# Turning maxima, context and two normed inputs with 32x32 block transposes and DMA instead of TensorE

## Chip, cores and metric

One Trainium2 chip, one core. The metric is the device time of one launch in microseconds (us), lower is better. Engines are named TensorE (PE), VectorE (DVE), ScalarE (ACT), GpSimd (POOL) and SyncE (SP, which issues all DMAs here).

## What is computed

A decoder block in float32 on 64 sequences of 256 tokens with 256 features, 16 heads of 16. `ctx_1024` has 120 rows per sequence. Cut to what matters:

```python
def reference(x, ctx_1024, ...):                    # x (64, 256, 256), ctx (64, 120, 256)
    x = x + local_attention(_layernorm(x))          # each token sees 3 before and 3 after it
    x = x + cross_attention(_layernorm(x), ctx_1024, ctx_1024)
    h = _layernorm(x)
    h = h + causal_attention(rmsnorm(h, n1_w))
    h = h + moe(rmsnorm(h, n2_w))                   # softmax gate, silu(h @ up.T) @ down.T, width 1024
    return x + h
```

## The kernel before

Tokens lie on partitions in `x`, `y`, `xn` (two blocks of 128), features on partitions in `xT`, as the projections need them. The 64 sequences are independent. Five are under way at a time, each in a lane of its own (`LANES = 5`, one set of SBUF tensors per lane), so that TensorE can work for one while the others wait for other engines. Work is cut into named parts ("turn", "project", "max", ...), each on one engine.

**Parts of a sequence.** For each of the layers local (0), cross (1), causal (2) and feed-forward (3): "moments" (DVE, then POOL) and "norm" (ACT) make the normed input `xn`. "turn" transposes it: four 128x128 transposes on PE (L790) into PSUM, and an ACT copy to `xT` (L1028). The context is turned the same way by "turn_ctx" (L797, L1032) into `cT`. Local attention: "project_rows" (L810) for k, v, q, "send" and "fetch" through DRAM (L703, L719) to give each partition its window, products on POOL (L630, L635) and sums on DVE (L1361), "turn_out" (L925) and "project_out" (L939). Cross and causal attention: "project" (L832, L838), "max" (scores in one orientation on PE, L866, their maxima on DVE, L1407), "shift" (the maxima transposed on PE, L877, copied by DVE, L1411), "place" (two DMAs, L728, that write them as extra rows into `qT`), "scores" (L888, exponentials L1075), "values" (L911), "normalise" (DVE, L1418 to L1434, which turns blocks by itself) and "project_out". Feed-forward: "gate" (L950), "up" (L961), "down" (L970).

**Whole array and parts.** "max", "scores", "values" and "gate" use 32 rows or 32 columns of the PE array at a time (`tile_position`), four side by side. Everything else uses the whole array.

**What sets the order.** `Plan` makes the instruction order of each engine at build time, from durations written into the parts. On PE the order is that of the table `POSITION` (sequence number plus position), with free choice among the next 60 parts only in the fill and the drain. On the other engines a part that is ready is taken by its due time, shifted by the table `SHIFTED`. Each engine's queue is then fixed and in order. PSUM has 8 banks; parts on the array take four ("quad") or one ("single"). Where the plan sees PE wait over 1 us, it puts filler matmuls there, which compute nothing (L770):

```python
if now - stopped > LONG_WAIT and p.name != "derive":
    one = PASSING * (2 if warmth < WARMS_IN else 1)
    self.passing[p.name, n, p.args] = count = int((now - stopped - MARGIN) / one)
```

Of the kernel before, what the change touches and what calls it, by code (L numbers as in the profile page):

```python
# [7 lines left out]
P = 128  # L8
LANES = 5
# [8 lines left out]
DOTS = 6  # L18
SLOT = 32
# [39 lines left out]
def score_units(layer):  # L59
# [16 lines left out]
EASY_REJOIN = 0.13  # L76
WIRE = 330.0
LANDING = 1.1
COOLS_AFTER, WARMS_IN = 1.5, 3.4
EMPTIED = 0.24  # L80
# [3 lines left out]
EARLY = 0  # L84
EARLY_ON_DVE = {("window_times", (c,)): busy for c, busy in ((0, 0.92), (2, 0.65), (4, 0.65), (6, 0.8), (8, 0.7), (10, 0.7))}
BEHIND = {("weights", (3,), "SP"): ("fetch", ("k",), "SP", 0), ("weights", (4,), "SP"): ("fetch", ("v",), "SP", 0)}

POSITION = {("turn", (0,)): -0.0773, ("turn_ctx", ()): -0.0394, ("project_rows", ("k",)): -0.0389, ("project_rows",
    ("v",)): 0.0516, ("project_rows", ("q",)): 0.0643, ("project", (1, "v")): 0.8052, ("turn_out", ()): 1.0641,
    ("project_out", (0,)): 1.2473, ("project", (1, "k")): 1.2641, ("turn", (1,)): 1.4729, ("project", (1, "q")):  # L90
    1.5195, ("max", (1, 0)): 1.6554, ("max", (1, 1)): 1.6713, ("shift", (1,)): 1.8861, ("scores", (1, 1)): 1.9724,
    ("scores", (1, 0)): 2.0874, ("values", (1,)): 2.3718, ("project_out", (1,)): 2.5298, ("turn", (2,)): 2.6364,
    ("project", (2, "k")): 2.7808, ("project", (2, "q")): 2.8094, ("max", (2, 0)): 2.8523, ("project", (2, "v")):
    2.899, ("max", (2, 1)): 3.0514, ("max", (2, 2)): 3.1338, ("shift", (2,)): 3.2929, ("scores", (2, 1)): 3.4513,
    ("scores", (2, 0)): 3.53, ("scores", (2, 2)): 3.6057, ("values", (2,)): 3.8413, ("project_out", (2,)): 3.9289,
    ("turn", (3,)): 4.2641, ("up", (0,)): 4.3625, ("up", (1,)): 4.3677, ("gate", ()): 4.4232, ("up", (2,)): 4.4727,
    ("up", (3,)): 4.4907, ("down", ()): 4.6197}

SHIFTED = {("down", (), "DVE"): -0.0629, ("fetch", ("k",), "SP"): 0.2, ("fetch", ("v",), "SP"): 0.5928, ("gate", (),
    "ACT"): 0.0687, ("load", (), "SP"): -0.8911, ("max", (1, 0), "DVE"): -0.0311, ("max", (1, 1), "DVE"): 0.0013,  # L100
    ("max", (2, 0), "DVE"): -0.4475, ("max", (2, 1), "DVE"): 0.4429, ("max", (2, 2), "DVE"): 0.7354, ("moments",
    (0,), "DVE"): 0.6903, ("moments", (0,), "POOL"): 0.9004, ("moments", (1,), "DVE"): -0.981, ("moments", (1,),
    "POOL"): 0.2012, ("moments", (2,), "DVE"): 0.0297, ("norm", (0,), "ACT"): -0.0134, ("norm", (0,), "POOL"):
    -0.2814, ("norm", (1,), "POOL"): 0.12, ("norm", (2,), "ACT"): -0.393, ("norm", (3,), "ACT"): 1.0224, ("norm",
    (3,), "POOL"): 0.1706, ("normalise", (2,), "DVE"): -0.0553, ("place", (1,), "SP"): -0.3445, ("project", (1,
    "q"), "ACT"): -0.8017, ("project", (1, "v"), "DVE"): 0.247, ("project", (2, "k"), "ACT"): 0.6832,
    ("project_out", (0,), "DVE"): 0.4817, ("project_out", (1,), "DVE"): -0.2502, ("project_out", (2,), "DVE"):
    -0.1622, ("project_rows", ("k",), "DVE"): -0.078, ("project_rows", ("v",), "DVE"): -0.3457, ("scores", (2, 0),
    "ACT"): 0.3209, ("scores", (2, 1), "ACT"): -0.4329, ("scores", (2, 1), "POOL"): -0.4149, ("scores", (2, 2),
    "ACT"): -0.8947, ("scores", (2, 2), "POOL"): 0.336, ("send", ("k",), "SP"): 1.8199, ("send", ("v",), "SP"):  # L110
    -0.087, ("shift", (1,), "DVE"): 0.0251, ("shift", (2,), "DVE"): -0.9285, ("store", (), "SP"): -0.0128, ("turn",
    (0,), "ACT"): 0.1725, ("turn", (1,), "ACT"): 0.1889, ("turn", (2,), "ACT"): 2.029, ("turn_ctx", (), "ACT"):
    0.021, ("turn_out", (), "ACT"): -0.1453, ("up", (0,), "ACT"): 0.4114, ("up", (0,), "DVE"): -0.5841, ("up", (1,),
    "ACT"): 0.026, ("up", (1,), "DVE"): 1.7562, ("up", (2,), "ACT"): 0.1018, ("up", (2,), "DVE"): 0.0745, ("up",
    (3,), "ACT"): -0.0954, ("up", (3,), "DVE"): -0.1548, ("weigh", (), "POOL"): 0.0496, ("window_exp", (), "ACT"):
    -0.0668, ("window_max", (), "DVE"): -0.5864, ("window_reduce", (0,), "DVE"): -0.0766, ("window_reduce", (1,),
    "DVE"): 0.8292, ("window_reduce", (2,), "DVE"): 0.0141, ("window_reduce", (3,), "DVE"): -0.3849,
    ("window_reduce", (4,), "DVE"): -0.1917, ("window_reduce", (5,), "DVE"): -0.5257, ("window_reduce", (6,),
    "DVE"): 0.384, ("window_reduce", (7,), "DVE"): -0.0381, ("window_reduce", (8,), "DVE"): 1.1728,
    ("window_reduce", (9,), "DVE"): 0.1471, ("window_reduce", (10,), "DVE"): 1.2711, ("window_reduce", (11,),  # L120
    "DVE"): -0.0619, ("window_times", (0,), "POOL"): 0.052, ("window_times", (2,), "POOL"): -0.0118,
    ("window_times", (3,), "POOL"): 0.1314, ("window_times", (4,), "POOL"): 1.461, ("window_times", (5,), "POOL"):
# [1391 lines left out]
```

## Time and profile before

| | |
|---|---|
| median of 3 runs | 3522.82 us (3520.79 to 3526.21) |
| the profiled execution, its time | 3523.18 us |
| its span | 3521.5 us |
| PE busy | 3464.6 us (98%) |
| POOL busy | 2498.7 us (71%) |
| ACT busy | 1828.8 us (52%) |
| DMA, mean | 63 GB/s |
| granted clock | 0.999 |

A row of the timeline gives the start in us from the span's start, the length, engine, line, operation, output and inputs, shapes, and how many instructions it merges. A float32 matmul is recorded as two, so x8 is four matmuls. Matmuls overlap, and a row's length holds some of the next one's; the distance of two starts is what the work takes in the queue. In square brackets stands idle time of that engine before the row and what ended it.

### The profile page before, as it was taken

The page shows a single profiled execution, that of the slowest core. Times are in us where ns is not written, and L with a number is a line of the kernel's source. Part 1 is how long each engine was busy: PE and PEld are TensorE (multiplying, and loading weights), DVE is VectorE, ACT ScalarE, POOL GpSimd, SP SyncE. Part 2 cuts the span into 40 slices and gives each one's busy share as a digit, 9 for nine tenths or more (in the row PEclk, how much of TensorE's full clock was granted, in tenths as well). Part 3 has the DMA queues.
Part 4 walks back from the last instruction along what each step waited for, and adds up shares of the span by engine and source line. Part 5 has one row for each costly group of instructions (what it writes and reads, how often), then busy time and mean ns, then how long its engine had stood idle before and what let it go on. Part 6 is the DMA issues. An engine that isn't in the chain of part 4 may idle for free.

```text
span 3521.5 us, 92506 instructions
## 1 busy us (share of the span) xinstructions
PE 3464.6 (98%) x36557; PEld 2788.9 (79%) x36557; DVE 2674.4 (76%) x5867; ACT 1828.8 (52%) x4241; POOL 2498.7 (71%) x3160
## 2 busy tenths in 40 slices
PE   8899999999999999999999999999999999999998
PEld 5577888888888888888888888888888888888876
DVE  5677787787787787787787787787787787787763
ACT  3344555555555555555545545545545545545542
POOL 5767777777777777777777777777777777777731
PEclk9999999999999999999999999999999999999999
DMA  5111221121121121221121221221221121121200
GB/s 182 50 51 50 70 73 51 68 74 51 68 74 52 67 74 50 69 74 50 66 77 47 69 77 46 69 77 47 69 77 47 69 77 47 69 77 47 69 8 10
DMA packets 90151, 223.35 MB, mean 63 GB/s; under 512 B 9286, under 2 KB 56706, under 8 KB 73346
## 3 DMA queue, kind: packets, MB, share of 16 engines
q1 hardware_dynamic: 89730, 217.44, 18.1%
q8 instruction: 300, 4.92, 0.6%
q14 instruction: 121, 0.99, 0.1%
HBM read 164.92 MB, written 50.39 MB: 61 GB/s over the span
## 4 chain that ended last, share of the span: by engine, by line
PE 94%; POOL 2%; ACT 2%; DVE 2%; issue 1%; SPq 0%; DMA 0%; DVEq 0%; POOLq 0%; ACTq 0%
PE ps L970 13%; PE ps L961 13%; PE ps L832 11%; PE ps L810 10%; PE ps L888 9%; PE ps L939 9%; PE ps L866 9%; PE ps L911 8%; PE ps L838 5%; PE ps L790 3%; PE ps L860 1%; PE ps L877 1%; ACT prob L1075 1%; PE ps L925 1%; POOL chunks L635 1%; DVE nmax L1407 1%
## 5 line engine op out<-in xcount | busy, mean ns | idle before, releaser
L635 POOL TENSOR_TENSOR chunks<-v_windows,xT 128x560 f32<-128x560 f32 (+1 forms) x384 | 879.6, 2301 | 92.2 <-DVE xT L1382 89.2
L1407 DVE TENSOR_REDUCE nmax<-ps 128x4 f32<-128x480 f32 (+2 forms) x1280 | 776.9, 671 | 182.8 <-PE ps L866 182.6
L1075 ACT ACTIVATE prob<-ps 128x256 f32<-128x256 f32 (+2 forms) x1536 | 670.7, 556 | 457.7 <-PE ps L888 457.5
L630 POOL TENSOR_TENSOR chunks<-rest,k_windows 128x512 f32<-128x512 f32 (+1 forms) x384 | 552.2, 1455 | 373.9 <-DMA k_windows<-passed_on 301.1
L1361 DVE TENSOR_REDUCE held<-chunks 128x80 f32<-128x560 f32 (+1 forms) x384 | 294.6, 768 | 321.2 <-POOL chunks L635 319.8
L961 PE MATMUL ps<-xT,w_up 128*128 128x256 f32 x2048 | 480.3, 383 | 1.4 <-ACT xT L1028 1.3
L970 PE MATMUL ps<-w_down,held 128*128 128x256 f32 x2048 | 459.1, 382 | 1.1 <-DVE held L1460 1.0
L970 PEld LDWEIGHTS ps<-w_down,held 128*128 128x128 f32 x2048 | 383.8, 190 | 60.1 <-DVE held L1460 2.8
L961 PEld LDWEIGHTS ps<-xT,w_up 128*128 128x128 f32 x2048 | 372.4, 190 | 69.4 <-issue 20.6
L1232 POOL TENSOR_SCALAR_AFFINE_SELECT prob<-prob 128x512 f32<-128x512 f32 x512 | 311.3, 642 | 50.6 <-ACT prob L1075 50.6
L1028 ACT COPY xT<-ps 128x512 f32<-128x512 f32 x256 | 152.9, 597 | 361.6 <-PE ps L790 361.6
L1361 DVE TENSOR_REDUCE xT<-chunks 128x32 f32<-128x512 f32 (+1 forms) x384 | 291.9, 760 | 21.8 <-POOL chunks L630 21.7
L911 PE MATMUL ps<-prob,va 120*32 120x256 f32 (+2 forms) x6144 | 303.5, 346 | 4.2 <-ACT prob L1075 2.0
L911 PEld LDWEIGHTS ps<-prob,va 120*32 120x32 f32 (+1 forms) x6144 | 179.7, 110 | 122.4 <-issue 45.9
L866 PE MATMUL ps<-held 32*128 32x120 f32 (+2 forms) x4096 | 260.2, 321 | 3.2 <-ACT held L1045 2.4
L888 PE MATMUL ps<-held 32*128 32x128 f32 (+2 forms) x3072 | 241.4, 380 | 10.0 <-issue 4.6
L1204 POOL TENSOR_TENSOR x<-x,y 128x512 f32<-128x512 f32 x64 | 81.4, 1272 | 233.8 <-DVE y L1444 233.8
L1016 ACT ACTIVATE held<-x,nmean,rstd 128x256 f32<-128x256 f32 x256 | 140.0, 595 | 186.0 <-POOL nmean L1179 186.0
L1108 ACT ACTIVATE rest<-ps 128x512 f32<-128x512 f32 x256 | 154.7, 604 | 115.9 <-PE ps L961 115.9
L888 PEld LDWEIGHTS ps<-held 32*128 32x128 f32 (+1 forms) x3072 | 123.1, 181 | 97.2 <-issue 90.1
L1460 DVE SCALAR_TENSOR_TENSOR held<-rest,ps 128x512 f32<-128x512 f32 x256 | 172.7, 675 | 23.1 <-ACT rest L1108 22.4
L1418 DVE STREAM_TRANSPOSE ps<-ps 128x512 f32<-128x512 f32 x256 | 170.1, 707 | 20.0 <-PE ps L911 19.3
(152 smaller groups left out, 6783.8 us busy)
## 6 DMA issues: line engine op xcount, KB each, us to landing
k_windows<-passed_on SPq DMA_DIRECT2D x64, 1024.0 KB, 5.0
v_windows<-passed_on SPq DMA_DIRECT2D x64, 1024.0 KB, 5.0
x<-in_x SPq DMA_DIRECT2D x64, 256.0 KB, 2.9
passed_on<-rest SPq DMA_DIRECT2D x64, 256.0 KB, 2.3
passed_on<-held SPq DMA_DIRECT2D x64, 256.0 KB, 3.7
out<-x SPq DMA_DIRECT2D x64, 256.0 KB, 2.2
y<-in_ctx SPq DMA_DIRECT2D x64, 120.0 KB, 2.9
held<-nmaxT SPq DMA_DIRECT2D x256, 8.0 KB
```

The source lines that it names most:

```text
L630: return engine.tensor_tensor(chunk_of(c).rearrange("p (j d) -> p j d", d=D), token_rows["q"][s][:, b, :].unsqueeze(1).to_broadcast([P, n, ...
L635: return engine.tensor_tensor(chunk_of(c).rearrange("p (h i j) -> p h i j", i=HD, j=WINDOW), window("v", b * D + first * HD, (HD, n), (1, ...
L810: last = nc.tensor.matmul(ps[:, b, tb * D:(tb + 1) * D], tokens, W[f"local_{w}"][:, k, :], start=(k == 0), stop=(k == 1))
L832: last = nc.tensor.matmul(ps[:, b, m * n:(m + 1) * n], wt[:, k, m * P:(m + 1) * P], src[:, k, 0:n], start=(k == 0), stop=(k == 1))
L866: last = nc.tensor.matmul(ps[:, to[r], place * keys:(place + 1) * keys], qT[s][e][rows, m, tb * P:(tb + 1) * P], kT[L][s][e][rows, m, 0:keys],
L888: last = nc.tensor.matmul(ps[0:keys, to[r], n * qs:(n + 1) * qs], kT[L][s][e][rows, m, key0:key0 + keys], qT[s][e][rows, m, q0:q0 + qs], s ...
L911: last = nc.tensor.matmul(ps[SLOT * j:SLOT * (j + 1), b, e * T + q0:e * T + q0 + qs], va[s][0:keys, kb, head:head + SLOT], pr[0:keys, j, c ...
L961: last = nc.tensor.matmul(ps[:, b, m * T:(m + 1) * T], w_up[:, k, (2 * m2 + m) * P:(2 * m2 + m + 1) * P], xT[s][:, k, :], start=(k == 0), ...
L970: last = nc.tensor.matmul(ps[:, b, tb * D:(tb + 1) * D], hid[s][:, m, tb * P:(tb + 1) * P], w_down[:, m, :], start=(m == 0), stop=(m == F ...
L1075: last = nc.scalar.activation(prob_pair(seq, L, m)[0:keys, :, r, col:col + qs], of_pair, ACT.Exp, scale=SCALE)
L1361: nc.vector.tensor_reduce(to, chunk_of(c).rearrange("p (x i) -> p x i", i=width), AX_X, ALU.add).then_inc(reduced[s], 1)
L1407: nc.vector.tensor_reduce(of_heads[:, ms[0]:ms[-1] + 1, :, r], src, AX_X, ALU.max, negate=True).then_inc(emptied[b], 1)
```

## The change

- `BY_DMA = ("ctx", 1, 3)`: the context and the normed inputs of cross and feed-forward are no longer turned on PE. ACT writes the normed rows in 32-feature blocks. "flip" (DVE) transposes all 32x32 blocks in place. "spread" (SP) writes them to a DRAM tensor with features as rows, in 8 DMAs (4 for the context) whose pieces are 32 tokens, 128 B. "gather" (SP) waits for all of them and reads 256 features by 256 tokens back into `xT` (or `cT`) in one DMA. The turns of layers 0 and 2 stay on PE.
- "shift" loses its PE transpose: DVE writes the maxima into `max_blocks`, transposes its 32x32 blocks, and "place" takes 8 DMAs instead of 2.
- `POSITION` and `SHIFTED` are new, which gives every engine another order. Code for doing window products on DVE, which was switched off (`EARLY = 0`), is gone.

```diff
+BY_DMA = ("ctx", 1, 3)
+FLIP, SPREAD_KB = 0.56, 1000
...
-POSITION = {("turn", (0,)): -0.0773, ("turn_ctx", ()): -0.0394, ("project_rows", ("k",)): -0.0389, ("project_rows",
...
+POSITION = {("turn", (0,)): 2.982, ("project_rows", ("k",)): 3.1458, ("project_rows", ("v",)): 3.1965,
...
+    def by_dma(what, after, flip, hops, spread_kb, kb):
+        a = part("flip", (what,), "DVE", flip, after)
+        a = part("spread", (what,), "SP", hops * DMA_ISSUE, [a, of_ctx] if what == LOCAL and of_ctx else [a],
+                 lag=LANDING, kb=spread_kb)
+        return part("gather", (what,), "SP", DMA_ISSUE, [a], lag=LANDING, kb=kb)
...
-            a = through("shift", (layer,), 0.2, "DVE", 0.4, last)
-            shifted = part("place", (layer,), "SP", 2 * DMA_ISSUE, [a], lag=2.0)
+            a = part("shift", (layer,), "DVE", 0.2, last)
+            shifted = part("place", (layer,), "SP", 8 * DMA_ISSUE, [a], lag=1.6)
...
-                        wait_taken(sp, "shift", seq, L)
+                        sp.wait_ge(flipped[s], reached["flipped", "shift", seq, (L,)])
                         for e in range(2):
-                            to = qT[s][e][16 * (1 - e):P:32]
-                            sp.dma_start(to, nmaxT[s][8 * e:8 * e + 8, :]).then_inc(placed[s], 16)
+                            to = qT[s][e][16 * (1 - e):P:32].rearrange("r m (b i q) -> r m b i q", b=2, q=SLOT)
+                            for i in range(4):
+                                first = SLOT * i + 4 * e
+                                sp.dma_start(to[:, :, :, i, :], nmaxT[s][first:first + 4, :]).then_inc(placed[s], 16)
+                    elif name == "spread":
+                        what, = args
+
+                        sp.wait_ge(flipped[s], reached["flipped", "flip", seq, args])
...
+                            to = features[s].rearrange("(x f) t -> f x t", f=SLOT)
+                            for tb in range(2):
+                                for i in range(4):
+                                    first = tb * P + i * SLOT
+                                    sp.dma_start(to[:, :, first:first + SLOT], xn_blocks[s][SLOT * i:SLOT * (i + 1), :, tb]
+                                                 ).then_inc(spread[s], 16)
+                    elif name == "gather":
+                        what, = args
+
+                        sp.wait_ge(spread[s], reached["spread", "spread", seq, args])
...
+                            sp.dma_start(xT[s][:], features[s].rearrange("(k p) t -> p k t", p=P)).then_inc(gathered[s], 16)
...
-                    elif name == "shift":
-                        L, = args
-                        wait_taken(pe, "max", seq, L, len(max_fills(L, T, C)) - 1)
-                        b = bank(name, seq, args)
-                        for tb in range(2):
-                            last = nc.tensor.transpose(ps[0:H, b, tb * P:(tb + 1) * P], nmax[s][:, tb, :], ident[:])
-                        last.then_inc(filled[b], 1)
...
+                    elif name == "flip":
+                        what, = args
+                        if what == "ctx":
+                            dve.wait_ge(ctx_loaded[s], reached["ctx_loaded", "load", seq, ()])
+                            rows = cx[s]
+                        else:
+                            dve.wait_ge(xn_ready[s], reached["xn_ready", "norm", seq, (what,)])
+                            rows = xn_blocks[s].rearrange("p x b f -> p (x b f)")
+                        nc.vector.transpose(rows, rows).then_inc(flipped[s], 1)
...
-                        b = bank(name, seq, args)
-                        nc.vector.tensor_copy(nmaxT[s][:], ps[0:H, b, 0:T]).then_inc(emptied[b], 1)
+                        L, = args
+                        for f in range(len(max_fills(L, T, C))):
+                            wait_taken(dve, "max", seq, L, f)
+                        nc.vector.transpose(nmaxT[s][:], max_blocks[s][:].rearrange("p m b h -> p (m b h)")).then_inc(
+                            flipped[s], 1)
```

How the queues move is read from the orders. The numbers behind names are lanes. PE, a steady round before, from the causal maxima past the causal output projection (L939 with `xT0`; L877 is the shift, L790 a turn, L797 the context's turn):

```order
L866 MATMUL ps<-rest1,held1 128x128 x4
L877 MATMUL ps<-ident,nmax2 16x128 x2
L838 MATMUL ps<-w_causal_v,xT1 128x256 x4
L790 MATMUL ps<-ident,held4 128x128 x4
L939 MATMUL ps<-w_causal_o,xT0 128x256 x4
L797 MATMUL ps<-ident,y4 128x120 x2
L810 MATMUL ps<-w_local_k,xT4 128x256 x4
L888 MATMUL ps<-held2 120x256 x4
```

PE now, from the causal output projection of lane 4 (L991 is the old L939, L869 the old L810, L849 the old L790, L919 and L925 masks and maxima, L940 scores, L977 the old L925, L897 the old L838):

```order
L849 MATMUL ps<-ident,held3 128x128 x4
L991 MATMUL ps<-w_causal_o,xT4 128x256 x4
L869 MATMUL ps<-w_local_k,xT3 128x256 x4
L919 MATMUL ps<-mask_rows,pick_rows 128x4x32 x16
L925 MATMUL ps<-held0 128x128 x4
L925 MATMUL ps<-rest0,held0 128x128 x4
L925 MATMUL ps<-held0 128x128 x4
L925 MATMUL ps<-rest0,held0 128x128 x4
L897 MATMUL ps<-w_cross_v,y2 120x256 x2
L869 MATMUL ps<-w_local_v,xT3 128x256 x4
L977 MATMUL ps<-ident,held2 128x128 x4
L919 MATMUL ps<-mask_rows,pick_rows 128x2x32 x16
```

Behind these rows come maxima, one unit of scores, the local output projection, a unit of scores, masks and maxima, the local q projection and the cross values, and then the gate and "up" of lane 4. Before, a turn of lane 0 stood between the causal output projection and "up", and the gate came after half of "up". A round has one context turn, two turns and two shifts fewer on PE. It goes from whole-array work into parts eight times (one of them straight from rows to columns inside), six times before. The whole order has 1093 changes of this kind against 927, and 429 fillers against 328, of which 18 stood ahead of the first projection and none do now.

SP, one round before (L732 store, L696 and L697 load, L728 place, L703 send, L719 fetch):

```order
L732 DMA out<-x3 128x2x256
L696 DMA x3<-in_x 128x2x256
L697 DMA y3<-in_ctx_1024 120x256
L728 DMA held1<-nmaxT1 4x2x256 x2
L703 DMA passed_on<-rest3 128x512
L719 DMA k_windows<-passed_on 128x2048
L703 DMA passed_on<-held3 128x512
L719 DMA v_windows<-passed_on 128x2048
L728 DMA held0<-nmaxT0 4x2x256 x2
```

SP now, from the first place of a round to the store (L757 place, L775 spread, L785 gather, L789 store; load, the context's spread in 4 and its gather follow):

```order
L757 DMA held4<-nmaxT4 4x4x32 x8
L733 DMA passed_on<-rest1 128x512
L746 DMA k_windows<-passed_on 128x2048
L775 DMA features<-held2 32x8x32 x8
L733 DMA passed_on<-held1 128x512
L785 DMA xT2<-features 128x2x256
L746 DMA v_windows<-passed_on 128x2048
L757 DMA held3<-nmaxT3 4x4x32 x8
L775 DMA features<-held0 32x8x32 x8
L785 DMA xT0<-features 128x2x256
L789 DMA out<-x2 128x2x256
```

A round had 11 DMAs and has 46. The fetch of the v windows now stands behind the gather of a feed-forward input.

VectorE before, from the addition of the causal output (L1444) through its moments:

```order
L1444 TENSOR_TENSOR y0<-y0,ps 128x512
L1327 TENSOR_TENSOR rest4<-ps,b_local_k 128x512
L1316 BN_STATS stats0<-y0 128x6 x2
L1319 BN_AGGR mv0<-stats0 128x2 x2
L1407 TENSOR_REDUCE nmax1<-ps 128x2 x4
```

VectorE now, from the same addition (L1495) to the flip of that input (L1389):

```order
L1495 TENSOR_TENSOR y1<-y1,ps 128x512 [waits filled5]
L1376 BN_STATS stats1<-y1 128x6 [waits emptied5]
L1376 BN_STATS stats1<-y1 128x6
L1379 BN_AGGR mv1<-stats1 128x2 [waits dve_step]
L1379 BN_AGGR mv1<-stats1 128x2
L1396 TENSOR_TENSOR rest0<-ps,b_local_k 128x512 [waits filled4]
L1409 TENSOR_REDUCE held4<-chunks1 128x80 [waits multiplied4]
L1455 TENSOR_REDUCE max_blocks2<-ps 128x2x2 [waits filled0]
L1455 TENSOR_REDUCE max_blocks2<-ps 128x2x2 [waits filled1]
L1455 TENSOR_REDUCE max_blocks2<-ps 128x2x2 [waits filled2]
L1455 TENSOR_REDUCE max_blocks2<-ps 128x2x2 [waits filled3]
L1389 STREAM_TRANSPOSE held1<-held1 128x512 [waits xn_ready1]
```

The flip stands behind a window sum and four reductions of another lane's maxima.

## Rows read from the trace of the kernel before

**Rows 1.** The page: busy time by engine, and the chain that ended last.
```profile
PE 3464.6 (98%) x36557; PEld 2788.9 (79%) x36557; DVE 2674.4 (76%) x5867; ACT 1828.8 (52%) x4241; POOL 2498.7 (71%) x3160
...
PE 94%; POOL 2%; ACT 2%; DVE 2%; issue 1%; SPq 0%; DMA 0%; DVEq 0%; POOLq 0%; ACTq 0%
```

**Rows 2.** Timeline of PE, in the fill and in a steady round (start, length).
```profile
97.10 0.71 PE L888 MATMUL ps<-held 32*120 32x256 f32 x8
97.63 0.61 PE L888 MATMUL ps<-held,y 32*120 32x256 f32 x8
98.06 0.61 PE L888 MATMUL ps<-held 32*120 32x256 f32 x8
...
1504.27 0.39 PE L877 MATMUL ps<-ident,nmax 128*16 128x128 f32 x2
1504.49 1.89 PE L838 MATMUL ps<-w_causal_v,xT 128*128 128x256 f32 x8
1506.22 0.60 PE L790 MATMUL ps<-ident,held 128*128 128x128 f32 x4
1506.66 1.89 PE L939 MATMUL ps<-w_causal_o,xT 128*128 128x256 f32 x8
1508.39 0.37 PE L797 MATMUL ps<-ident,y 120*128 120x120 f32 x2
1508.60 1.90 PE L810 MATMUL ps<-w_local_k,xT 128*128 128x256 f32 x8
1510.43 0.71 PE L888 MATMUL ps<-held 32*120 32x256 f32 x8
...
1512.07 0.61 PE L866 MATMUL ps<-rest,held 32*128 32x256 f32 x8
1512.61 2.00 PE L810 MATMUL ps<-w_local_v,xT 128*128 128x256 f32 x8
1514.45 0.60 PE L925 MATMUL ps<-ident,held 128*128 128x128 f32 x4
...
1525.97 1.93 PE L911 MATMUL ps<-prob,va 120*32 120x256 f32 x32
```

**Rows 3.** Timeline of PE, the first projection and the longest run of fillers.
```profile
12.85 1.97 PE L810 MATMUL ps<-w_local_k,xT 128*128 128x256 f32 x8 [0.72 <-issue]
...
55.49 15.92 PE L770 MATMUL ps<-ident_b 128*128 128x512 bf16 x73
```

**Rows 4.** Timeline, from the causal output's addition to the normed feed-forward input.
```profile
1509.49 0.68 DVE L1444 TENSOR_TENSOR y<-y,ps 128x512 f32<-128x512 f32 x1
...
1513.85 0.91 ACT L1023 ACTIVATE held<-y,rrms 128x256 f32<-128x256 f32 x2
```

**Rows 5.** Timeline of DVE, block transposes in PSUM and in SBUF.
```profile
1502.59 1.32 DVE L1418 STREAM_TRANSPOSE ps<-ps 128x512 f32<-128x512 f32 x2
...
1504.74 0.76 DVE L1434 STREAM_TRANSPOSE xT<-held 128x256 f32<-128x256 f32 x2
```

**Rows 6.** DMA: the page's issues to landing, an issue on SP, place's issues (min/median/max ns).
```profile
x<-in_x SPq DMA_DIRECT2D x64, 256.0 KB, 2.9
passed_on<-rest SPq DMA_DIRECT2D x64, 256.0 KB, 2.3
...
5.90 0.43 SPq L682 DMA_DIRECT2D w_local_q<-in_local_q  x1
...
L728 SPq DMA_DIRECT2D held<-nmaxT x256: 520/527/601, 94.7 to 3465.6; - x128
```

**Rows 7.** DMA packets from 38 to 41 us, then from 41 to 44 us.
```profile
DMA packets 923, 1.12 MB, mean 373 GB/s; under 512 B 18, under 2 KB 860, under 8 KB 923
q1 hardware_dynamic: 923, 1.12, 105.4%
...
DMA packets 1019, 0.94 MB, mean 313 GB/s; under 512 B 474, under 2 KB 656, under 8 KB 1019
q1 hardware_dynamic: 1019, 0.94, 91.4%
```

More of the change, by code:

```diff
@@ L99 @@
[L99 to L122, printed above, removed]
-    -0.0845, ("window_times", (6,), "POOL"): -0.067, ("window_times", (7,), "POOL"): 0.5659, ("window_times", (9,),
-    "POOL"): -1.4167, ("window_times", (10,), "POOL"): 0.4511, ("window_times", (11,), "POOL"): -0.926}
@@ L194, in sequence_parts @@
         added = [part("norm", (layer,), "POOL", 1.37, [normed])] if layer < CAUSAL else []
-        turned = through("turn", (layer,), 0.44, "ACT", 0.49, [normed])
+        if layer in BY_DMA:
+            turned = by_dma(layer, [normed], FLIP, 8, SPREAD_KB, 256)
+        else:
+            turned = through("turn", (layer,), 0.44, "ACT", 0.49, [normed])
         if layer == LOCAL:
@@ L260, in sequence_parts @@
     added = part("norm", (3,), "POOL", 1.23, [done])
-    turned = through("turn", (3,), 0.44, "ACT", 0.49, [normed])
+    if 3 in BY_DMA:
+        turned = by_dma(3, [normed], FLIP, 8, SPREAD_KB, 256)
+    else:
+        turned = through("turn", (3,), 0.44, "ACT", 0.49, [normed])
     gated = ("gate", (), "PE")
@@ L289 @@
            ("scores", "POOL"): {"masked": 1},
-           ("place", "SP"): {"placed": 32},
+           ("shift", "DVE"): {"flipped": 1},
+           ("flip", "DVE"): {"flipped": 1},
+           ("place", "SP"): {"placed": 128},
+           ("gather", "SP"): {"gathered": 16},
            ("normalise", "DVE"): {"attended": 1},
@@ L313, in __init__ @@
         at = {p[:3]: i for i, p in enumerate(parts)}
-        early = {i: EARLY_ON_DVE[p[:2]] for i, p in enumerate(parts) if p[:2] in EARLY_ON_DVE and p.engine == "POOL"}
         released = {(who[3], at[who[:3]]): at[what] for what, who in BEHIND.items()}
-        def engine_of(n, i):
-            return "DVE" if n < EARLY and i in early else parts[i].engine
         followers = defaultdict(list)
@@ L344, in offer @@
         def offer(n, i):
-            e = engine_of(n, i)
+            e = parts[i].engine
             if e != "PE":
@@ L410, in __init__ @@
                     self.order[e].append((p.name, n, p.args))
-                    busy = early[i] if e == "DVE" and i in early else p.busy
-                    end = now + busy
+                    end = now + p.busy
                     if e == "PE":
@@ L444, in __init__ @@
                 elif what == "free":
-                    idle.add(engine_of(n, i))
+                    idle.add(parts[i].engine)
                     j = released.get((n, i))
```

157 lines of the change are left out of this document (100 added, 57 removed).

## Prediction

> **What bounds the kernel now.** I read the page first. TensorE is busy 98% of the span and the chain that ended last lies on PE for 94% [rows 1]; VectorE has 76%, GpSimd 71%, ScalarE 52%. So a microsecond taken from PE's queue is worth a microsecond, as long as PE doesn't wait for something new, and work put on another engine or on the DMA queue is free until PE waits for it. Next the timeline of PE in the steady part: instructions overlap, so what one costs PE is read from start to start, not from its own length. A steady round (one sequence's worth of PE work) holds almost no idle time, and every row in [rows 2] follows the one before at once. Last come the first 100 us, in which PE has nothing to do and runs filler matmuls [rows 3], then the engines behind the turn of the feed-forward input, SP's issues and the DMA packets.
>
> **What is removed from PE.** Per sequence: two of the four turns of the normed input (cross and feed-forward), the turn of the context, and two shifts of the maxima. A turn takes 1506.66 - 1506.22 = 0.44 us, the context's 1508.60 - 1508.39 = 0.21, a shift 1504.49 - 1504.27 = 0.22 [rows 2]. Together 2 x 0.44 + 0.21 + 2 x 0.22 = 1.53 us, times 64 = **-98 us**. ScalarE also loses three copies per sequence and has room anyway.
>
> **What the new order adds on PE.** PE changes between matmuls over the whole array and matmuls on 32-row or 32-column parts (maxima, scores, values, gate), and each change costs. A projection takes 1.73 us between whole-array work (1506.66 to 1508.39), but 1.83 before parts (1508.60 to 1510.43) and 1.84 after them (1512.61 to 1514.45). The first part group takes 0.53 where the next takes 0.43 (97.10, 97.63, 98.06), and the last before a projection takes 1512.61 - 1512.07 = 0.54 [rows 2]. So going in costs about 0.20 and coming out about 0.22. A steady round of the old order has 6 stretches of parts, one of them left through a shift, which starts without the 0.10 of a projection; the new one has 8, as the order's rows show. Two more stretches are 2 x 0.42 = 0.84, the lost cheap exit is 0.10, and two joints fewer inside stretches give back about 0.28. That is +0.66 us per round, 42 us in 64; the fill and drain have a little less of it (the whole order has 1093 changes against 927, so 26 fewer than three more per round): **+37 us**. Nearly 40% of the gain goes here.
>
> **Fill and drain.** The number of fillers rises from 328 to 429. One takes 15.92 / 73 = 0.218 us [rows 3]. Of the old ones, 18 stood ahead of the first projection at 12.85 us, where PE waited for a load in any case. So 119 more stand in the way, 119 x 0.218 = 26 us, and without the early ones the first projections start on a cold engine, some 2 us: **+28 us**. This is a longer first passage: where a turn took a PE pass and a copy (0.44 and 0.6), the first sequences now go through DRAM twice.
>
> **The DRAM turn, on the path or beside it.** In the steady state it is paid only if the turned input comes later than PE reaches it. The tightest place is the feed-forward input. In the new order the gate follows the causal output projection after three row projections and an output projection (6.92), cross values' projection 0.87, a turn of 0.44, two score units (1.72), three sets of maxima with their masks (3.0, at 0.43 for a group of 256 columns, half for 128, 0.1 to 0.2 for a mask) and the cross values (1.7, their 1.93 less the overlap with the next): 14.7 us, plus three ways in and out and one into columns, 1.4: **16.1 us** [rows 2]. Against it stands the chain. From the end of that projection at 1508.39 to the normed input at 1513.85 + 0.91 = 1514.76 it was 6.4 us, with VectorE's queue in it (the addition starts 1.1 us late) [rows 4]. Then the block transpose: 128x512 in SBUF has no row; the nearest are 0.66 us from PSUM (1.32 for two) and 0.38 for 128x256 in SBUF (0.76 for two) [rows 5], so 0.38 to 0.76; I take 0.66. Then 8 issues on SP at 0.43 [rows 6], or as long as their pieces take: a DMA is 256 pieces of 128 B, 16 per DMA engine. With 1 KB pieces a packet costs 3 x 16 x 1.054 / 923 = 0.055 us. In the stretch where 474 of 1019 are under 512 B, taking the others at 0.055 leaves 43.9 - 30.0 = 13.9 us, 0.029 us each [rows 7]. So a DMA takes 0.46 us, about what its issue takes. The bounds are issue alone, 3.4 us for eight, and 0.055 a piece, 7.0 us; I take 3.7, since 128 B is nearer the small ones. Landing after the last issue is 2.3 - 0.4 = 1.9, and the gather costs 2.9 like the load of x, the same 256 KB [rows 6]. With 0.5 us for signals the chain is 6.4 + 0.7 + 3.7 + 1.9 + 2.9 + 0.5 = **16.1 us**: a tie. Four reductions of maxima (2.5 us) stand ahead of the flip on VectorE, and SP's next jobs wait behind the gather's wait.
>
> The other places have more room. The cross input has about 25 us of PE work between its output projection and its use, against a chain of 16. The context is loaded most of a round before use. The placing of the maxima loses the shift and its copy and gains a 128x128 transpose (about 0.3), but is 8 issues instead of 2. At the 0.53 us that such an issue takes [rows 6] that is 4.2 instead of 1.1, 3.1 us later; for the cross layer this leaves about 1 us. SP in all: 46 issues per round at 0.43 to 0.53, some 22 us of 52. VectorE: 2674 + 64 x (2 x 0.66 + 0.38 + 2 x 0.3) = 2821 us, 80% of the time, before two small copies are taken off. None of these is a bound, but with two ties and a fuller VectorE I count 0.25 us of waiting per round, between 0 and 1.2: **+16 us**.
>
> **Sum.** 3523.2 (the profiled execution; the median of the runs, 3522.8, is the same) - 98 + 37 + 28 + 16 = 3506 us, 0.5% less.
>
> **Rivals.**
> - *Late gate (slower).* The same chain takes over 16.1 us and PE waits in front of the gate in every round. It decides from 0.5 us on, since the sum leaves 17 us besides 0.25 per round. At 1.3 us the waits are 83 us and the time is 3573. For it speaks that no step has slack; against it that PE waits almost nowhere today, although its order was as tight.
> - *Small writes to DRAM are slow.* The small packets above, at 0.029, need not be writes to DRAM. If a write of 128 B took twice the 1 KB price, 0.11 us, a spread is 14 us, the gate is 10 us late and the time about 4150. The Trainium skill (DMA: Bandwidth & Descriptors, Specifications) states that pieces under 512 B miss the line rate since the engine reads, changes and writes them. By it this rival would be the case; no row of this trace shows such writes.
> - *Late placing.* The eight issues leave the cross scores 0.5 us late at each round: 3506 + 32 = 3538.
> - *More is kept.* The waits vanish and the ways in and out cost 0.5 per round: 3506 - 16 - 10 = 3480.
> - *Nothing is left.* The saved 98 us are given back in full by changes, fill and small waits of 0.5 per round: 3522.
>
> **How the numbers follow.** Forecast (3490 to 3515) 0.46; more is kept 0.12; nothing left 0.14; late gate 0.18; late placing 0.06; slow writes 0.04. A measurement of this kernel tells 0.2% (7 us) from no change. Faster is 0.46 + 0.12 = 0.58, same 0.14, slower 0.18 + 0.06 + 0.04 = 0.28. The likeliest case gives 3506. The range goes down to 3470 (more kept, and a shorter fill) and up to 3567 (1.2 us of waiting per round), which leaves out the slow writes and half of the late gate.
>
> **What would show it.** In the changed profile a steady round, from one down projection to the next, should be shorter than before by 1.53 - 0.66 - 0.25 = 0.6 us; turns on PE halved, no context turn or shift; fillers 429. Waits of PE's gate group for a DMA of xT should sum to under 20 us; over 60 would be the late gate. A spread DMA's pieces near 0.03 us each keep it; at 0.1 the slow writes rule. The forecast is wrong if the round isn't shorter, or if the first down projection comes over 40 us later than before.

## The result: slower by 0.3%, and the profile after

| | before | after |
|---|---|---|
| median | 3523.37 us (3519.40 to 3530.48, 20 runs) | 3535.43 us (3522.16 to 3542.33, 20 runs) |
| ratio | | 1.0031, 95% interval 1.0022 to 1.0040 |
| profiled execution: time, span | 3523.18, 3521.5 us | 3540.67, 3539.0 us |
| mean granted clock | 0.999 | 0.997 |

The time lies in the range, but on the wrong side of before: forecast 3506. The page of the changed kernel, whose first two lines answer to [rows 1]; then DMA packets and issues with the median time to landing:

```profile
PE 3432.0 (97%) x35762; PEld 2726.7 (77%) x35762; DVE 2793.3 (79%) x6069; ACT 1726.2 (49%) x4049; POOL 2501.9 (71%) x3160
...
PE 67%; DVE 10%; DMA 10%; SPq 7%; issue 3%; ACT 3%; POOL 1%; DVEq 0%; ACTq 0%; POOLq 0%
```
```profile
DMA packets 507958, 306.35 MB, mean 87 GB/s; under 512 B 396358, under 2 KB 474498, under 8 KB 491138
...
k_windows<-passed_on SPq DMA_DIRECT2D x64, 1024.0 KB, 5.2
...
features<-held SPq DMA_DIRECT2D x1024, 32.0 KB, 2.0
xT<-features SPq DMA_DIRECT2D x128, 256.0 KB, 2.7
```

PE is 33 us less busy and ends 17.5 us later. The chain that ended last was 94% PE and is 67% now; DVE, DMA and SP's issues hold 27%. The waits of PE say where (total us, times, longest):

```profile
PE ps L1002 <- DMA xT<-features: 30.6, 24, 2.8
PE ps L940 <- ACT prob L1132: 22.5, 63, 1.0
...
PE ps L940 <- DMA held<-nmaxT: 4.0, 4, 1.5
```

L1002 is the gate, which waits for the gathered feed-forward input; L940 the cross scores, which wait 0.33 us for ScalarE in nearly every round. Before, the gate waited for no DMA, and the scores' waits for ScalarE came to 3.0 us. The timeline of PE at the third, 58th and 64th down projection splits the loss by stage, first before, then after:

```profile
322.82 0.48 PE L970 MATMUL ps<-w_down,held 128*128 128x256 f32 x1
...
3232.97 0.48 PE L970 MATMUL ps<-w_down,held 128*128 128x256 f32 x1
...
3508.96 0.48 PE L970 MATMUL ps<-w_down,held 128*128 128x256 f32 x1 [0.61 <-DVE held L1460]
```
```profile
321.00 0.48 PE L1022 MATMUL ps<-w_down,held 128*128 128x256 f32 x1
...
3232.50 0.48 PE L1022 MATMUL ps<-w_down,held 128*128 128x256 f32 x1
...
3526.29 0.48 PE L1022 MATMUL ps<-w_down,held 128*128 128x256 f32 x1 [0.62 <-DVE held L1511]
```

The fill is 1.8 us shorter. The 55 steady rounds are 2910.1 us before and 2911.5 after, although the undisturbed round, the length to which rounds return again and again, fell from 52.74 to 52.09 (left aside is one of 52.45 before, right behind the fill). The last six rounds (the drain) grew from 276.0 to 293.8, by 17.8. So two questions: what took back the steady gain, and what lengthened the drain.

A late round, on SP (the last row is from the list of SP's waits in the whole run) and then on PE; the third fence is PE by stretch (length, busy, granted clock, DMA share, GB/s):

```profile
2091.59 0.34 SPq L746 DMA_DIRECT2D k_windows<-passed_on  x1
2091.98 4.07 SPq L775 DMA_DIRECT2D features<-held  x8
2096.09 2.30 SPq L733 DMA_DIRECT2D passed_on<-held  x1
2100.41 0.38 SPq L785 DMA_DIRECT2D xT<-features  x1
...
SPq L746 <- DMA passed_on<-rest: 96.6, 59, 3.1
```
```profile
2104.21 0.43 PE L1002 MATMUL ps<-xT,w_gate 128*32 128x64 f32 x16 [2.78 <-DMA xT<-features]
2104.57 8.64 PE L1013 MATMUL ps<-xT,w_up 128*128 128x256 f32 x31
```
```profile
2104.00:2106.00 2.00, 1.79 (x20) 0.69 0.62 246
2106.00:2108.00 2.00, 2.00 (x7) 0.50 0.25 45
2108.00:2116.00 8.00, 8.00 (x49) 0.99 0.25 57
```

Right ahead of the eight spreads SP issues the 1 MB fetch of the next k windows. The last spread is issued at 2096.05, the gather only at 2100.41: 4.4 us, where the 31 steady rounds that are on time take 1.2 to 2.7. The fetch stands in this place in all 55 steady rounds; why 24 of them are late and the others not stays open. It also holds SP's queue, since it waits there for its own data (the row L746): in the median the spreads start 0.6 us behind the end of the flip. And behind the 2.78 us of waiting the granted clock is at its lower level (0.50, 1.2 GHz) for a while, so 31 recorded matmuls of the up projection take 8.64 us, where 32 take 7.2 in other rounds. Four of the 24 late gates, with waits of 1.8 to 2.8 us, are followed by such a stretch.

### The profile page after: what moved, and what is told of

It reads as the page before. It is cut to its first block, busy times and chain, and to the rows that moved or that the text cites. A ratio compares the mean times of both kernels' runs of the same rounds, so it can differ in the third digit from the quotient of the medians.

```text
span 3539.0 us, 93364 instructions
## 1 busy us (share of the span) xinstructions
PE 3432.0 (97%) x35762; PEld 2726.7 (77%) x35762; DVE 2793.3 (79%) x6069; ACT 1726.2 (49%) x4049; POOL 2501.9 (71%) x3160
## 2 busy tenths in 40 slices
DMA packets 507958, 306.35 MB, mean 87 GB/s; under 512 B 396358, under 2 KB 474498, under 8 KB 491138
## 4 chain that ended last, share of the span: by engine, by line
PE 67%; DVE 10%; DMA 10%; SPq 7%; issue 3%; ACT 3%; POOL 1%; DVEq 0%; ACTq 0%; POOLq 0%
PE ps L1022 13%; PE ps L1013 13%; PE ps L891 7%; PE ps L940 7%; PE ps L869 6%; PE ps L925 5%; PE ps L991 5%; PE ps L963 5%; SPq L757 4%; DVE max_blocks L1455 3%; PE ps L897 3%; DMA features<-held 3%; SPq L775 3%; ACT prob L1132 2%; DMA xT<-features 2%
## 5 line engine op out<-in xcount | busy, mean ns | idle before, releaser
L1455 DVE TENSOR_REDUCE max_blocks<-ps 128x4 f32<-128x480 f32 (+2 forms) x1280 | 774.9, 669 | 69.5 <-PE ps L925 68.8
L1013 PE MATMUL ps<-xT,w_up 128*128 128x256 f32 x2048 | 465.7, 386 | 0.1
L1013 PEld LDWEIGHTS ps<-xT,w_up 128*128 128x128 f32 x2048 | 388.2, 192 | 57.8 <-issue 0.7
L1233 POOL TENSOR_SCALAR ms<-mv 128x2 f32<-128x2 f32 x192 | 42.2, 220 | 501.3 <-DVE mv L1379 490.8
L1409 DVE TENSOR_REDUCE xT<-chunks 128x32 f32<-128x512 f32 (+1 forms) x384 | 283.1, 763 | 28.7 <-POOL chunks L658 28.3
L1080 ACT ACTIVATE held<-y,rrms 128x256 f32<-128x256 f32 x256 | 116.1, 500 | 331.1 <-POOL rrms L1246 329.0
L940 PE MATMUL ps<-held 32*128 32x128 f32 (+2 forms) x3072 | 238.1, 378 | 28.4 <-ACT prob L1132 22.5
L925 PE MATMUL ps<-held 32*128 32x120 f32 (+2 forms) x4096 | 258.5, 321 | 2.8 <-ACT held L1102 1.6
L940 PEld LDWEIGHTS ps<-held 32*128 32x128 f32 (+1 forms) x3072 | 124.5, 181 | 126.1 <-issue 119.6
L925 PEld LDWEIGHTS ps<-held 32*128 32x128 f32 x4096 | 162.4, 186 | 34.7 <-issue 30.1
```

The lines of the kernel that those rows point to most:

```text
L925: last = nc.tensor.matmul(ps[:, to[r], place * keys:(place + 1) * keys], qT[s][e][rows, m, tb * P:(tb + 1) * P], kT[L][s][e][rows, m, 0:keys],
L940: last = nc.tensor.matmul(ps[0:keys, to[r], n * qs:(n + 1) * qs], kT[L][s][e][rows, m, key0:key0 + keys], qT[s][e][rows, m, q0:q0 + qs], s ...
L1013: last = nc.tensor.matmul(ps[:, b, m * T:(m + 1) * T], w_up[:, k, (2 * m2 + m) * P:(2 * m2 + m + 1) * P], xT[s][:, k, :], start=(k == 0), ...
L1409: nc.vector.tensor_reduce(to, chunk_of(c).rearrange("p (x i) -> p x i", i=width), AX_X, ALU.add).then_inc(reduced[s], 1)
L1455: nc.vector.tensor_reduce(of_heads[:, ms[0]:ms[-1] + 1, :, r], src, AX_X, ALU.max, negate=True).then_inc(emptied[b], 1)
```

## Experiments

The theory was contention with that fetch; the rival a chain that is too long by itself. All times are medians; each ratio is to runs of before on the same chip (3522.2 to 3523.4).

**1. The k fetch behind the spreads.** SP's order only:

```diff
+        sp = self.order["SP"]
+        for n in range(N):
+            i = sp.index(("fetch", n, ("k",)))
+            for j in range(i + 1, min(i + 3, len(sp))):
+                if sp[j][0] == "spread" and sp[j][2] == (3,):
+                    sp.insert(j, sp.pop(i))
+                    break
```

> Edit: in each round SP's fetch of the k windows (1 MB) is moved from just ahead of the eight feed-forward spreads to just behind them; the other engines' orders are those of the change. Theory 1 (contention): in the change, PE's gate group waits 30.6 us in 24 rounds for the gathered features, because the 1 MB fetch goes first and its packets share the DMA engines with the spreads (an issue of eight spreads takes 3.9 to 5.2 us instead of 3.7) and with their landing. Then the spreads issue in 3.7 to 4.2 us, the gather goes out within 2.5 us of the last one, the gate waits sum to under 10 us, the rounds with a clock loss behind such a wait go, and the time is about 3500 to 3515 (20 to 35 below the change). Theory 2 (the chain is too long by itself, VectorE's flip or the spreads' own issue): the waits stay over 25 us and the time is 3530 to 3540.

Measured: 3599.1 us, 1.0212 (1.0195 to 1.0229). Neither range was met. SP's timeline and PE's wait (lines are 7 further down):

```profile
2339.85 4.90 SPq L782 DMA_DIRECT2D features<-held  x8
2344.85 0.39 SPq L753 DMA_DIRECT2D k_windows<-passed_on  x1
2345.29 0.43 SPq L740 DMA_DIRECT2D passed_on<-held  x1
2345.96 0.37 SPq L792 DMA_DIRECT2D xT<-features  x1
```
```profile
PE ps L1009 <- DMA xT<-features: 76.5, 58, 2.1
```

The spreads are now done 1.2 us after the last issue, so that half of the theory holds. But the gather has the fetch ahead of it and takes 5.8 us to land in this round, 2.7 in the median of the change. The gate is now late in nearly every round (54 of the 55 steady ones, 24 before this edit). In the 53 steady rounds of which both landings are recorded, the gather lands 1.2 us or more behind the fetch, though it is issued only 1.1 us after it. The fetch harms whatever stands behind it.

**2. The k fetch behind the gather too.** As 1, with the search going on to the `gather` of layer 3.

> Edit: the same fetch moved behind the gather of the feed-forward features as well, so that neither spreads nor gather share the DMA engines with it. Theory 1 (contention): as with the fetch behind the spreads, or up to 10 us better, since there the gather still runs beside the fetch; gate waits under 5 us, time 3495 to 3515. The price would be seen at GpSimd's convolution, which gets its k windows some 3 to 6 us later. Theory 2 (chain too long by itself): 3530 to 3540, gate waits over 25 us. If the fetch behind the gather makes the windows late, GpSimd waits for k_windows and PE's row projections of the next round are late: over 3540.

Measured: 3503.0 us, 0.9946 (0.9933 to 0.9958), 32 us below the change and 19 below before. SP, from the same place of a round:

```profile
2388.49 5.00 SPq L782 DMA_DIRECT2D features<-held  x8
2393.54 0.45 SPq L740 DMA_DIRECT2D passed_on<-held  x1
2394.70 0.38 SPq L792 DMA_DIRECT2D xT<-features  x1
2395.18 0.41 SPq L753 DMA_DIRECT2D k_windows<-passed_on  x1
```
```profile
POOL chunks L665 <- DMA k_windows<-passed_on: 97.9, 58, 3.9
```

In the steady rounds the gate no longer waits for the gather. The same DMAs in another order are worth 37 us in the steady rounds (2874.4 against 2911.5; the profiled execution of the change was 5 us slower than its median, so by medians it is 32). The edit takes away the fetch's bytes and its 0.6 us hold on SP's queue together. The landing of the last spread fell from 2.3 us in the median to 1.2, so the bytes are the larger part; no run takes away one without the other. The price is where it was looked for: GpSimd waits 97.9 us for its windows, and nothing on PE notices.

**3. Some slack on PE as well.** As 1, and the self-attention turn put behind the causal output projection: `("turn", (0,)): 2.99`.

> Edit: the fetch behind the spreads, and the remaining PE turn of the self-attention input put behind the causal output projection instead of ahead of it, so that the gate comes 0.44 us later after that projection with the same work in a round. Theory 1 (contention): little is left to gain, within 5 us of the kernel with the fetch behind the spreads alone. Theory 2 (the chain is too long by itself): 0.44 us of slack takes away waits of 0.44 us in each of the some 24 late rounds, about 10 us and the clock losses of the shortest: 3515 to 3530, and clearly below the kernel without the slack.

Measured: 3624.0 us, 25 above experiment 1. The gate's waits are shorter, but nothing is gained. The maxima behind the turn come later on PE, VectorE reduces them ahead of the flip, and the flip ends 9.42 us behind the projection's start instead of 8.2; and the local projection now waits for the turn's copy:

```profile
PE ps L1009 <- DMA xT<-features: 51.2, 54, 1.5
PE ps L876 <- ACT xT L1092: 35.5, 50, 2.4
```

So the edit did not test the slack alone. What it does show is that PE work put ahead of a chain that is fed by PE moves the chain's start too.

**4. The feed-forward input turned on PE again.** `BY_DMA = ("ctx", 1)` and `("turn", (3,)): 7.365`.

> Edit: the feed-forward input is turned by PE matmuls again (0.44 us of PE per round, 28 us in all), maxima, context and cross input stay with DRAM; the planner then needs 390 fillers instead of 429 (8.5 us less). Theory 1 and 2 agree that the gate's waits for a DMA go altogether; what is measured is their whole price with the clock losses. If the late gate with its clock loss costs what I read (about 36 us more excess over the shortest round than before), the time is 3535 - 36 + 28 - 8 = 3519, and the drain is shorter. If the waits cost only their own 30.6 us: 3524. If the loss is elsewhere (the last five rounds, 18.7 us longer, and the waits at the scores), it is 3530 or over.

Measured: 3511.8 us, 0.9970 (0.9959 to 0.9982). No gate waits. That is 7 us under the 3519 expected from the late gate's whole price. Its shortest round is 52.44 us: the turn costs 0.35, not 0.44, which is 6 us in 64 rounds. The last six rounds are 286.7 us, 7.1 less than the change.

**5. The maxima alone.** `BY_DMA = ()`, `("turn", (1,)): 4.67`, `("turn_ctx", ()): 3.32`, turn 3 as in 4.

> Edit: all turns (context, cross and feed-forward inputs) on PE again; of the change only the maxima's block transpose and the eight placing DMAs stay, with the new order's eight stretches of parts in a round. By the forecast's own terms the maxima alone save two shifts (0.44 us a round) and cost two more stretches (0.66): +14 us, and the 392 fillers of this order are 64 more than before, 18 of which the old order had where they cost nothing: +10 to +18. Expected 3523 + 14 + 14 = 3551, and no wait of the gate for a DMA. If the price of the ways in and out was overestimated, so that the maxima pay for themselves, it is under 3535. Its last five rounds, against the kernel with only the feed-forward turn on PE, tell how much of the longer drain is the placing's and how much the cross input's.

Measured: 3516.3 us, 0.9982 (0.9973 to 0.9990), 35 below the expectation. Its undisturbed round is 52.71, next to 52.74 before. With two turns and the context back it is only 0.62 above the change, where their rows add up to 2 x 0.44 + 0.21 = 1.09. The timeline of PE shows one reason; first this kernel, then the change, from the local output projection to the second pair of cross scores:

```profile
2354.68 1.98 PE L991 MATMUL ps<-w_local_o,xT 128*128 128x256 f32 x8
2356.50 0.37 PE L856 MATMUL ps<-ident,y 120*128 120x120 f32 x2
2357.00 0.71 PE L940 MATMUL ps<-held 32*120 32x256 f32 x8
```
```profile
2361.34 0.71 PE L940 MATMUL ps<-held 32*120 32x256 f32 x8 [0.33 <-ACT prob L1132]
```

The scores start 2.32 us behind the projection in the one, with the context's turn in between, and after 0.33 us of waiting for ScalarE in the other. In this order the turn's place is free.

**6. A quarter of the bytes.** As 1, the k fetch cut to 256 KB:

```diff
+                        cut = HELD * D // (4 if w == "k" and seq else 1)
-                        sp.dma_start(windows[w][:],
-                                     bass.AP(src.tensor, src.offset, [[2 * D, P], [1, HELD * D]])).then_inc(
+                        sp.dma_start(windows[w][:, 0:cut],
+                                     bass.AP(src.tensor, src.offset, [[2 * D, P], [1, cut]])).then_inc(
```

> Edit: the order with the k fetch between spreads and gather (3599 us), but the fetch carries a quarter of its bytes for every sequence but the first (256 KB instead of 1 MB; the rest of the k windows isn't renewed, so the local layer's scores are not the reference's). There the time from the gather's issue to the gate was 5.5 to 7.1 us, where the change's undisturbed rounds have 2.7. Theory 1 (the gather waits for the bytes of the fetch ahead of it): the 2.8 to 4.4 us more shrink to a quarter, 0.7 to 1.1, the gate waits fall under 10 us in all and the time to 3495 to 3515. Theory 2 (a fixed price for any DMA between them, or for SP's order): the gather still takes over 5 us, waits of 60 to 80 us, 3580 or more.

Measured: 3500.3 us, 0.9935 (0.9921 to 0.9948), 99 below experiment 1 in the same order of DMAs:

```profile
PE ps L1010 <- DMA xT<-features: 1.0, 2, 0.7
```

The number of DMA packets is that of the change and of experiment 1, and only the bytes are fewer (they have 306.35 MB):

```profile
DMA packets 507958, 256.80 MB, mean 73 GB/s; under 512 B 396358, under 2 KB 474498, under 8 KB 499202
```

The time depends on the bytes ahead of the gather. The gather takes 4.2 us to land in the median of the steady rounds, against 3.0 with the fetch behind it (experiment 2) and 5.8 with 1 MB ahead (experiment 1). So 1.2 of the 2.8 us are left with a quarter of the bytes, a little over the 0.7 to 1.1 expected, and not all of it goes with the fetch's bytes (the 256 KB write `passed_on<-held` also stands just ahead).

**7. Cross scores earlier.** As 2, and `("scores", (1, 1)): 5.309`, to remove the 0.33 us wait.

> Edit: the k fetch behind the gather (3503 us), and the first pair of cross scores put one set of maxima earlier in PE's order, so that ScalarE's exponentials of it are done when the second pair comes. In each round PE waits 0.33 us there for ScalarE (22.5 us in 63). Theory: the wait goes, 12 fillers more cost 2.6 us: 3482 to 3490. Rival (late placing): the placed maxima land about when the earlier scores start (the last placing DMA is issued at 2386.6 us and lands some 1.6 later, the earlier place of the scores is at 2388.5), so PE waits for the placing instead, 0.2 to 1 us a round: 3495 to 3540.

Measured: 3534.8 us, 1.0035 (1.0022 to 1.0047). The wait for ScalarE went, but another took its place, and not the one named: not the placing, but VectorE, whose reductions of the maxima free the PSUM banks.

```profile
PE ps L947 <- DVE max_blocks L1462: 43.4, 61, 0.7
```

**8. Half of the placing.** As 2, four of the eight placing DMAs for every sequence behind the first five.

> Edit: the k fetch behind the gather (3503 us), and of the eight placing DMAs of each layer only four, for every sequence behind the first five (half of the maxima are then those of the sequence before in the lane, so the output isn't the reference's). A place takes SP 4.6 us, of which 2.3 go. Theory (placing lengthens the drain): the steady round stays 52.1 us and the last five rounds, 240 us with one of 61.5, get 5 to 12 us shorter, as two to five places lie on the chain there: 3491 to 3498. Rival (the drain is longer for the fillers and the order's gaps on PE): under 2 us shorter, 3501 to 3505.

Measured: 3501.5 us, 0.9941 (0.9928 to 0.9955); the last six rounds 293.0 us instead of 293.8. The expectation failed. But the fillers in the drain are fixed work, and stay even if what they cover gets shorter; so 10 and 11.

**9. The context on PE again.** As 2, `BY_DMA = (1, 3)` and `("turn_ctx", ()): 3.32`.

> Edit: the k fetch behind the gather (3503 us), and the context turned on PE again, between the two pairs of cross scores, where the kernel before has it; maxima and both inputs stay with the new ways. Forecast's term: the turn costs PE 0.21 us a round, +13 us: 3516. Theory (its place was free): in that place PE waits 0.33 us for ScalarE in every round once the turn is gone, so a round stays within 0.05 of 52.10 us and the wait at the scores shrinks from 22.5 us to under 8; with 439 fillers for 429 the time is 3500 to 3508.

Measured: **3498.3 us, 0.9928 (0.9916 to 0.9941)**, the fastest of all, 25 us below before and 37 below the change. It is 4.7 us below 2; that is under what a comparison can tell (7 us), but its slowest run is faster than the fastest of 2. (The expectation says that the kernel before has the turn there; it has it behind the causal output projection, [rows 2].) Its shortest round is 52.14 us, so the turn costs PE 0.05. The third down projection starts 5.7 us earlier than in 2; that the first contexts' shorter way is the reason is only argued.

The turn's place, and what is left of the wait:

```profile
2384.63 0.37 PE L863 MATMUL ps<-ident,y 120*128 120x120 f32 x2
2385.12 0.71 PE L947 MATMUL ps<-held 32*120 32x256 f32 x8
```
```profile
PE ps L947 <- ACT prob L1139: 2.6, 4, 1.0
```

**10 and 11. No fillers in the drain, and with half of the placing.** `if seq < B - 6 else 0` behind the count of fillers, on 2 and on 8.

> Edit: the k fetch behind the gather (3503 us), and the 149 fillers of PE in the last rounds left out (the kernel before has 80 there). Theory 1 (the fillers themselves lengthen the drain): PE finds its inputs nearly ready, and the last six rounds, 293.8 us against 276.0 of the kernel before, come 10 to 25 us shorter: 3478 to 3493. Theory 2 (the fillers stand where PE would wait in any case, for chains through the placing and the gathers): the drain stays within 5 us, with waits in the fillers' stead, and may get longer by a lower granted clock behind the waits: 3498 to 3515.

> Edit: as the kernel without fillers in the drain, and four of the eight placing DMAs of each layer left out for every sequence behind the first five (the maxima in their place are old ones, so the output isn't the reference's). If the placing's eight issues lengthen the drain, this is 5 to 12 us below the kernel without drain fillers: with fillers in the way, halving the placing had moved nothing (3501.5 against 3503.0). If they don't, it is within 2 us of it.

Measured: 3509.1 us, 0.9962 (0.9949 to 0.9976), and 3506.2 us, 0.9949 (0.9935 to 0.9962). Waits stand where fillers stood, and the clock falls. In the kernel of 10, PE's waits and its stretches in the drain:

```profile
PE ps L1009 <- DMA xT<-features: 13.0, 1, 13.0
PE ps L947 <- DMA held<-nmaxT: 12.3, 4, 8.8
```
```profile
3350.00:3400.00 50.00, 37.35 (x478) 0.97 0.13 28
3400.00:3450.00 50.00, 38.81 (x400) 0.86 0.08 17
3450.00:3496.00 46.00, 28.72 (x207) 0.81 0.07 18
```

With fillers the clock is 1.00 in all three. The last sequence's gate waits 13.0 us in one piece for its input to come back through DRAM; in the change 68 fillers stand in that place:

```profile
3502.49 14.85 PE L829 MATMUL ps<-ident_b 128*128 128x512 bf16 x68 [0.78 <-DVE y L1495]
3517.27 0.43 PE L1002 MATMUL ps<-xT,w_gate 128*32 128x64 f32 x16
```

The last six rounds of 10 are 298.9 us, 5 longer than with fillers, and the time is 6 us longer (its fastest run is slower than the slowest of 2). So the fillers don't lengthen the drain; they stand where PE waits in any case. Half of the placing is 2.9 us of the time, under what can be told, and 3.5 us of the last six rounds. It may be a small part of the drain's loss; it is not most of it.

**12. 9 and 10 together.**

> Edit: context on PE again, the k fetch behind the gather, no fillers in the drain: the candidate for the fastest. The effects add up if each is what it is taken for: the time is that of the kernel without drain fillers plus what the context's turn on PE cost with fillers (0 to +5 us, or less than 0 if the drain gets shorter without the context's way through DRAM); by theory 1 on the drain some 3480 to 3492, by theory 2 3497 to 3512.

Measured: 3501.2 us, 0.9936 (0.9923 to 0.9948). With the fillers, in 9, it was 3 us less, which is under what can be told; the two effects add up to 3509.1 - 4.7 = 3504.4, 3 us above what came.

By the same three down projections, the profiled execution of each kernel against that of before, in us. The profiled execution of 1 was 13 us faster than its median, those of the change and of 8 were 5 us slower, and the others lie within 3 us of theirs:

| kernel | fill | 55 steady rounds | drain |
|---|---|---|---|
| the change | -1.8 | +1.4 | +17.8 |
| 1, fetch behind spreads | -0.2 | +41.8 | +20.8 |
| 2, fetch behind gather | -2.4 | -35.7 | +17.8 |
| 3, 1 with slack on PE | +4.9 | +75.9 | +21.3 |
| 4, feed-forward turn on PE | +0.8 | -22.5 | +10.7 |
| 5, maxima alone | -4.4 | -10.1 | +7.4 |
| 6, 1 with a quarter of the bytes | -2.7 | -39.4 | +17.5 |
| 7, 2 with cross scores earlier | -0.4 | -7.0 | +19.0 |
| 8, 2 with half of the placing | -0.4 | -33.8 | +17.0 |
| 9, 2 with the context on PE | -8.1 | -40.0 | +20.3 |
| 10, 2 without fillers in the drain | +0.6 | -38.5 | +22.9 |
| 11, 8 without fillers in the drain | -1.2 | -36.4 | +19.5 |
| 12, 9 without fillers in the drain | -6.2 | -36.7 | +21.5 |

## Why the prediction was wrong

- **Where the miss lies.** By the forecast's own terms 55 steady rounds come 55 x (1.53 - 0.66 - 0.25) = 34 us shorter; they came 1.4 longer. All of the miss is in them. Fill and drain were to be +17 us together (the rest of the sum of -17), and are +16.
- **Idle time in a round: the failed step.** Forecast 0.25 us a round; the late gate alone took (2911.5 - 2874.4) / 55 = 0.67, 30.6 us of it as waits, and the rest about what the mean clock lost (0.997 for 0.999 is 7 us). By medians it is 32 / 55 = 0.59. The rival "late gate" named mechanism and place, and its threshold of 0.5 was passed; I gave it 0.18. Its signs came only in part: it said every round, and 24 of 55 were late; it said waits of over 60 us, the forecast under 20, and 30.6 came, between the two.
- **Why it was late.** The forecast compared a chain of 16.1 us with 16.1 us of PE work, both from the end of the causal output projection, called it a tie, and used prices of transfers with nothing ahead of them. In 2, with the fetch out of the way, the chain is shorter than forecast. From the start of that projection, 1.7 us before its end, it takes in the median flip 8.2, spreads 4.6, landing 1.2 and gather 3.0, 17.2 us in all (15.9 in the quickest rounds), against 18.5 us to the gate. Counted from the end as the forecast did, that is 15.5 against 16.8: 1.3 us of slack, no tie. What ate it was never in the sum: what SP's queue holds ahead of the chain. I counted SP's issues, but neither the bytes of the DMAs that are issued just ahead nor that one of them may wait there for its data (0.6 us). A 1 MB fetch takes about 5 us to land, 5.0 in the median before and 5.2 after. The Trainium skill (DMA: Bandwidth & Descriptors, Queues, rings and completion order) says that each DMA engine consumes descriptors in ring order, and that the semaphore increment lands only after every earlier write from that engine. By that rule a small DMA behind the fetch is told as done only when the fetch's part on its engine is; experiments 1, 2 and 6 agree with it (5.8, 3.0 and 4.2 us in the median for the same gather). They don't tell waiting in one ring from sharing of the engines; the fetch was not issued from another queue.
- **What PE saves in an undisturbed round.** Forecast 1.53 - 0.66 = 0.87; measured 52.74 - 52.09 = 0.65. Most of the missing 0.2 is the context's turn, which was costed at 0.21 and whose removal saved only 0.05, since PE waits 0.33 for ScalarE in its place (5, 9). In 9, 1.32 us less of turns and shifts make the undisturbed round 0.60 shorter, so the changes between whole array and parts cost 0.72: the term of 0.66 was about right. In whose account they fall was not: the maxima alone break even (5), and the two input turns are worth 0.57 together instead of 0.88. That an easy exit from the parts goes with them is argued from the order (in 5 a turn stands right behind the maxima) and not shown.
- **Fill and drain.** That their sum came out right is luck, as the parts were wrong. The fill got 1.8 us shorter in spite of 32 more fillers (280 for 248; ahead of the first projection the trace of before has 14, not 18). The first down projection came 8.4 us later than before, far from the 40 that was named as a sign. The drain got 17.8 longer: 7.4 with the maxima and the new order, 3.3 with the cross and context turns, 7.1 with the feed-forward turn (5, 4, 2). The 149 fillers there (80 before) stand for the latency of ways through DRAM with no other sequence to hide them; without them it is waits and a lower clock. What makes up the maxima's 7.4 stays open.
- **The likeliest number came in another kernel.** Experiment 2 has 3503 us, where the forecast was 3506, and its steady rounds are 35.7 us shorter, where 34 was forecast. That is in part luck too: it has almost none of the 0.25 us of waiting, and saves 0.2 less.
- **Spreads and small writes.** The eight took 3.8 us to issue in the quickest rounds (3.7 forecast) and 1.2 more to land: the slow writes of the rival did not come. A packet of 128 B took 0.013 us in the median, less than half of the 0.029 that was forecast. The Trainium skill (DMA: Bandwidth & Descriptors, Specifications) says that pieces under 512 B miss the line rate, and in that the trace agrees: a packet of 1 KB took 0.046 us, so a byte is 2.3 times as dear in the small ones. But 16 of them per DMA engine are 0.2 us, and SP takes 0.47 to issue such a DMA, so the price stays hidden.
- **Late placing** did not decide: PE waited 4.0 us for it in all. That this rival's 3538 us is the number nearest to the measured 3535 is chance.

## What to carry to other kernels

When work is moved to DMAs, write down for each new DMA on a waited-for chain what its queue issued in the 5 us ahead, in bytes. A big transfer that nobody waits for soon belongs behind the small ones that PE waits for; here this order alone decided between 0.3% slower and 0.5% faster. And look at what PE would do in the place of a removed instruction: a small one that fills a wait is free, and its removal costs its replacement.

## What the runs showed that I had not expected

- The same DMAs in three orders gave 3503, 3535 and 3599 us; the gather took 2.6 to 7.1 us for the same 256 KB.
- After a single wait of 2.8 us the granted clock went to 0.69 and then 0.50 for 2 us stretches.
- The eight issues of a place take 4.6 us undisturbed (0.58 each), those of a spread 3.8 in the quickest rounds (0.47), and the spreads up to 7.0 while other transfers run.
